# A decoder layer on one core: in every attention step VectorE takes the row maximum ahead of the projections' banks

## The chip, the cores and the metric

The kernel runs on one core of a Trainium2 chip. The metric is the time of one execution on the device in microseconds (us). Inputs and outputs are fp32; matmuls take fp32r operands that are split into a high and a low part.

## The reference, cut to what matters

A decoder layer with pre-norm on x of 8 x 256 x 512: a retention block, then a cross-attention with 32 heads of 16, then a feed-forward with 8 experts and a shared part. The change lies in the cross-attention:

```
q = (x @ Wq).reshape(b, n, N_HEADS, HEAD_DIM)
k, v = jnp.split(ctx @ Wkv, 2, axis=-1)
...
q = apply_axial_rope(q, pos_map)
k = apply_axial_rope(k, ctx_pos_map)
scale = 1.0 / np.sqrt(HEAD_DIM).astype(np.float32)
logits = jnp.einsum('bqhd,bkhd->bhqk', q, k) * scale
w = jax.nn.softmax(logits, axis=-1)
attn = jnp.einsum('bhqk,bkhd->bqhd', w, v)
...
return attn @ Wout + bout
...
x = x + _L0_xattn_ref(_layernorm(x, axis=-1), ctx_1024, fside_BxSx2_0, ...)
```

## The kernel before, in words

The three blocks run one behind the other: retention to about 350 us, cross-attention from 354 to 731 us, feed-forward to the end. The cross-attention walks over the 8 sequences of the batch (g). Each is a pipeline that is spread over several turns: the loop `bodies` runs a body b for b = -1 to 9, and in a body the 16 steps i (T = 16) each do one piece for every sequence b + d with d in -2, -1, 0, 1 that is alive. Every engine has this same loop in its own instruction stream, in its own written order; nothing is planned at run time, and semaphores tie the engines together.

What a step holds on TensorE, in order (line 1290 on): `rows` of head pair p = i of the current sequence (L1185: four matmuls that give the logits with the queries in the partitions, into banks 0 and 1 of `b_rt`; it waits for the maximum of the step before), `logits` of the pair 8 steps back (L1197, transposed logits into banks 2 and 3 for ScalarE's exponential, L1526), the turning of finished values (even steps, L1218), the turning of negated maxima (steps 0, 4, 8, 12, L1224), `values` (odd steps, L1210), and then the projection parts that `PLAN` puts into this step (`use`, L1227).

The projections share two PSUM banks, `b_gm` 0 and 1. In the middle bodies 2 to 6 the order by step, bank in brackets, is: w1 (0) steps 0 to 2, k0 (1) steps 2 and 3, x0 (0) and x1 (1) step 4, k1 (0) step 5, q0 (1) steps 6 to 8, q1 (0) steps 8 to 10, o0 (1) and o1 (0) step 11, v0 (1) step 12, v1 (0) steps 13 and 14, w0 (1) steps 14 and 15. k, q and v are projections of the next sequence, x the transposes of its normalised input, o and w the transposes and the output projection of the sequence before. The first writer of a bank waits on TensorE (L1234) for the semaphore `gm_read` of what was in it before. Body 0 has no o and w, body 1 no w, body 7 no k, x, q and v, and bodies 8 and 9 have no `rows` and no maxima.

A bank is emptied in the step behind its last part: k and q by two VectorE multiplications with the rotation tables (`take`, L1356; `b_ac`, `b_bs`), w by a VectorE addition (L1362), v by ScalarE, and x and o by a ScalarE copy (high part) and then a VectorE subtraction (L1348, low part, `b_xl`), which frees the bank. k0 is so taken in step 4, x0 and x1 in step 5, k1 in 6, q0 in 9, q1 in 11, o0 and o1 in 12, w0 in 0, w1 in 3. Behind the takes of k and q, GpSimd (POOL) sums the products (L1598, L1599), ScalarE makes the high part (L1509), POOL the low part (L1604), and SyncE (SP) sends both to DRAM and loads them again as chunks of rows for the next body.

VectorE's other work in a step stands behind takes and maximum: the negated maxima (steps 3, 7, 11, 15, L1377), the group that scales finished values (even steps, L1386, L1388), statistics (steps 0, 1) and normalisation (steps 2, 3) of the next sequence, and the statistics for the last norm (steps 4, 5, L1396, L1399). In body 0, step 10, a split of weights (`low_weights`, L1469) stands ahead of everything.

Of the kernel before, what the change touches and what calls it, by code (L numbers as in the profile page):

```python
# [32 lines left out]
def as_f32(ap):  # L33

    return ap.bitcast(FP32)
# [929 lines left out]
def cross_attention(nc, X, Wa, Wb, first, csT, wb_dram, ctx_dram, bout_dram, pack_dram, ident, held, final, lead, ws_dram, gate_dram, const_dram, tri_dram):  # L965
# [6 lines left out]
    with ExitStack() as mem:  # L972
# [96 lines left out]
        def due(i, live, step):  # L1069

            return [d for d in live if i - d * T == step]

        def pairs(i, live, lag):
            return [(d, i - d * T - lag) for d in live if 0 <= i - d * T - lag < HP]

        def quads(i, live, lag):
            return [(d, (i - d * T - lag) // 2) for d in live if 0 <= i - d * T - lag < HP and (i - d * T - lag) % 2 == 0]
# [17 lines left out]
        def fresh(g):  # L1095
            return isinstance(g, int) and g <= 0
# [223 lines left out]
        def _(dve):  # L1320

            def bn_first(g):
                nc.vector.bn_stats(out=st[:, 0, :], in_=X[:, g * TB, :])
# [9 lines left out]
            def normalize(g, t):  # L1333
                if t == 0:
                    dve.wait_ge(rstd_done, g)
                last = nc.vector.tensor_scalar(xn[:, t, :], X[:, g * TB + t, :], mv[:, t, 0:1], rstd[:, t:t + 1], ALU.subtract, ALU.mult)
                if t == TB - 1:
                    last.then_inc(xn_done, 1)

            def take(g, what, n):  # L1340

                bank = BANK[what, n]
                src = gm[:, bank, :]
                a = slice(n % 2 * P, (n % 2 + 1) * P)
                if what in ("x", "o"):
                    high, low, done, ahead = (xh, xl, xh_done, 1) if what == "x" else (ah, al, ah_done, 0)
                    dve.wait_ge(done, g * 2 + (n + 1 - 2 * ahead))
                    nc.vector.tensor_tensor(low[:, :, a], src.rearrange("p (m s) -> p m s", s=P), as_f32(high[:, :, a]), ALU.subtract)\  # L1348
                        .then_inc(gm_read[bank], 1)
                elif what in ("k", "q"):  # L1350
                    dve.wait_ge(gm_mm[bank], uses(g, what, n))
                    if not (second(g) and what == "k"):
                        dve.wait_ge(lo_out[n], g * 32 + (-32 if what == "k" else -16))
                    for k, dst in enumerate((ac, bs)):
                        angle = csT[:, k, bass.ts(g, S)].rearrange("p (o s) -> p o s", o=1).to_broadcast([P, 2, S])
                        last = nc.vector.tensor_tensor(dst[:, :, n, :], src.rearrange("p (r s) -> p r s", s=S), angle, ALU.mult)  # L1356
                    last.then_inc(gm_read[bank], 1)
                elif what == "w":
                    dve.wait_ge(gm_mm[bank], uses(g, what, n))
                    dve.wait_ge(bias_added, g + 1)  # L1360
                    tile = X[:, g * TB + n, :]
                    nc.vector.tensor_tensor(tile, src, tile, ALU.add).then_inc(gm_read[bank], 1)  # L1362

            def maximum(g, p):
                dve.wait_ge(row_mm, g * HP + (p + 1))
                nc.vector.tensor_reduce(out=mx[:, :, 2 * p:2 * p + 2].rearrange("p t e -> p e t"),  # L1366
                                        in_=rt[:, 0:2, :].rearrange("p e (t s) -> p e t s", s=S), op=ALU.max, axis=AX.X).then_inc(mx_done, 1)

            def negate(g, k, own):

                dve.wait_ge(mx_done, g * HP + (4 * k + 5))
                part = mx[:, :, 8 * k:8 * k + 8]
                if fresh(g) and k == 0:
                    dve.wait_ge(presets, 3)
                else:
                    dve.wait_ge(mt_mm, g * 4 + k)
                own.step(nc.vector.tensor_scalar(nm[:, :, 0:8].bitcast(FP32R), part, -1.0, None, ALU.mult))  # L1377
                nc.vector.scalar_tensor_tensor(out=nm[:, :, 8:16], in0=part, scalar=-1.0, in1=nm[:, :, 0:8],
                                               op0=ALU.mult, op1=ALU.subtract).then_inc(nm_done, 1)

            def group(g, q, own):

                dve.wait_ge(attn_done, g * 8 + (q + 1))
                dve.wait_ge(nat_done, g * 8 + (q + 1))
                src = nat[:, 0:S].rearrange("p (q d) -> p q d", d=VW)
                own.step(nc.vector.reciprocal(rs[:, :], src[:, :, XD]))  # L1386
                dst = attn[:, :, 64 * q:64 * q + 64].rearrange("p t (h d) -> p t h d", h=4)
                nc.vector.tensor_tensor(dst, src[:, :, 0:XD].rearrange("p (t h) d -> p t h d", t=TB),  # L1388
                                        rs[:, :].rearrange("p (t h o) -> p t h o", t=TB, o=1).to_broadcast([P, TB, 4, XD]),
                                        ALU.mult).then_inc(attn_done, 1)  # L1390
# [19 lines left out]
            def body(b, live):  # L1410
                if isinstance(b, int):
                    own = Chain(dve, dve_own, base=counted["n"])
                else:
                    own = Chain(dve, dve_own, PER, b, counted["n"] - 2 * PER)
                for i in range(T):
                    if isinstance(b, int) and b == 0 and i == 10:
                        low_weights()
                    if isinstance(b, int) and b == B:
                        if i == 0:
                            lead_shift()  # L1420
                        if 6 <= i < 10:
                            lead_low(i - 6)
                    for step, what, n in ENDS:
                        for d in due(i, live, step + 1):
                            if not (fresh(b + d) and step < 0):
                                take(b + d, what, n)
                    for d, p in pairs(i, live, 0):
                        maximum(b + d, p)
                    for k in range(4):
                        for d in due(i, live, 4 * k + 3):  # L1430
                            negate(b + d, k, own)
                    for d, q in quads(i, live, LAGV + 1):
                        group(b + d, q, own)
                    for d in due(i, live, -16):
                        if not fresh(b + d):
                            bn_first(b + d)
                    for d in due(i, live, -15):
                        if not fresh(b + d):
                            statistics(b + d, own)
                    for t in range(TB):  # L1440
                        for d in due(i, live, -14 + t):
                            if not fresh(b + d):
                                normalize(b + d, t)
                    if not (isinstance(b, int) and b > B):
                        for d in due(i, live, 36):
                            final_first(b + d, own)
                        for d in due(i, live, 37):
                            final_statistics(b + d, own)
                if isinstance(b, int):
                    counted["n"] += own.n  # L1450
                else:
                    assert own.n == PER, own.n
                    counted["n"] += (B - 3) * PER

            def lead_shift():
                over(dve)
                dve.wait_ge(frstd_done, 2)
                nc.vector.scalar_tensor_tensor(out=lead.shift_by[:, 0:4], in0=fmean[:, 0:4], scalar=-1.0, in1=frstd[:, 0:4],
                                               op0=ALU.mult, op1=ALU.mult).then_inc(lead.shift_done, 1)

            def lead_low(t):
                dve.wait_ge(lead.xh_done, t + 1)
                at = slice(t * P, (t + 1) * P)
                nc.vector.tensor_tensor(lead.xl[0][:, :, at], gm[:, t % 2, :].rearrange("p (m s) -> p m s", s=P),
                                        as_f32(lead.xh[0][:, :, at]), ALU.subtract).then_inc(lead.xl_done, 1)

            def low_weights():
                dve.wait_ge(wh_done, 1)
                nc.vector.tensor_tensor(wl[:, 2, :], raw[:, :], as_f32(wh[:, 2, :]), ALU.subtract).then_inc(wl_done, 1)  # L1469
# [1097 lines left out]
```

## Time and profile before

| | |
|---|---|
| three runs | 1412.5, 3906.36, 1416.9 us; median 1416.9 |
| the profiled execution | 1415.07 us, its span 1413.3 us |
| mean granted TensorE clock | 0.98 |
| busy in the span | PE 94%, DVE 60%, POOL 36%, ACT 34% |
| from the first `rows` to the end of the cross-attention | 354.27 to 731 us |

Times in the profile are microseconds from the start of the span. PE is TensorE's matmuls, PEld its weight loads, DVE VectorE, ACT ScalarE, POOL GpSimd. In a timeline each line gives the start, the duration from the first start to the last end of the instructions that were merged into it, the engine, the source line, the operation, the output and the inputs. Matmul ends are modelled, so neighbouring matmuls overlap a little in it. A bracket gives the idle time of the engine ahead of the instruction and what ended it.

### The profile page before, as it was taken

How to read it: one execution, taken by the hardware profiler on the slowest of the kernel's cores; microseconds unless marked ns; L12 is line 12 of the kernel's file. 1: busy time of each engine (PE TensorE's matmuls, PEld its weight loads, DVE VectorE, ACT ScalarE, POOL GpSimd, SP SyncE). 2: the span in 40 equal slices, each digit the busy share in tenths (PEclk: the TensorE clock that was granted, in tenths of full speed). 3: DMA queues.
4: the chain of work that ended last, by engine and by line, in shares of the span. 5: the costliest groups of instructions: out<-in, count | busy, mean ns of one | idle time of the engine just before them, and what ended most of it. 6: DMA issues, size and time to landing. Idle time of an engine off the chain costs nothing. (4 is left out here: it accounts for less than half of the span.)

```text
span 1413.3 us, 24145 instructions
## 1 busy us (share of the span) xinstructions
PE 1330.8 (94%) x8442; PEld 1071.2 (76%) x8442; DVE 848.3 (60%) x1519; ACT 486.5 (34%) x764; POOL 508.7 (36%) x359
## 2 busy tenths in 40 slices
PE   7999999998899999999889999999999899999983
PEld 5777777776666766666557888888878899999972
DVE  6766666687888778887744666555561332222255
ACT  4222223243365665565655111111111233332220
POOL 1122222234543344333140028411160775554054
PEclk9999999999799999999999999999999999999997
DMA  7992000003654554456200014220000434452257
GB/s 263 319 323 86 0 0 0 0 16 121 181 165 147 157 165 134 144 148 186 75 24 0 23 41 152 106 94 23 23 23 30 187 138 141 152 201 75 71 154 237
DMA packets 85035, 159.83 MB, mean 113 GB/s; under 512 B 8576, under 2 KB 61952, under 8 KB 81536
## 3 DMA queue, kind: packets, MB, share of 16 engines
q1 hardware_dynamic: 78688, 124.19, 28.0%
q0 software_dynamic: 6272, 34.61, 6.9%
q8 instruction: 51, 0.84, 0.2%
q14 instruction: 24, 0.20, 0.0%
HBM read 109.22 MB, written 69.47 MB: 126 GB/s over the span
## 5 line engine op out<-in xcount | busy, mean ns | idle before, releaser
L1526 ACT ACTIVATE b_pf<-b_rt,b_zero 128x1024 f32<-128x1024 f32 x128 | 142.9, 1116 | 127.3 <-PE b_rt L1197 127.0
L1366 DVE TENSOR_REDUCE b_mx<-b_rt 128x4 f32<-128x1024 f32 x128 | 156.3, 1221 | 47.3 <-PE b_rt L1185 47.2
L2058 DVE SCALAR_TENSOR_TENSOR residual<-c_yp,c_shared,residual 128x512 f32<-128x512 f32 x144 | 103.8, 744 | 114.4 <-PE c_yp L43 108.6
L41 PE MATMUL c_fc<-c_xh,c_w 128*128 128x512 f32 x352 | 137.7, 391 | 0.0
L43 PE MATMUL c_fc<-c_xh,c_w 128*128 128x512 f32 x352 | 137.1, 389 | 0.0
L42 PE MATMUL c_fc<-c_xl,c_w 128*128 128x512 f32 x352 | 137.0, 389 | 0.0
L2196 ACT ACTIVATE c_s<-c_fc 128x512 f32<-128x512 f32 x44 | 26.3, 598 | 231.9 <-PE c_fc L43 220.9
L41 PE MATMUL c_fc<-c_ring,c_xTl 128*128 x312 | 105.3, 338 | 0.0
L43 PE MATMUL c_fc<-c_ring,c_xTh 128*128 x312 | 100.6, 322 | 0.0
L42 PE MATMUL c_fc<-c_ring,c_xTh 128*128 x312 | 100.5, 322 | 0.0
L1878 POOL TENSOR_TENSOR c_w<-c_wraw,c_zero 128x1536 fp32r<-128x1536 f32 x9 | 24.8, 2750 | 202.5 <-DMA c_wraw<-in_c_ws 108.5
L2072 DVE TENSOR_TENSOR c_hTl<-c_eh,c_hTh 128x384 fp32r<-128x384 f32 x39 | 21.7, 557 | 124.2 <-ACT c_hTh L2220 113.1
L1185 PE MATMUL b_rt<-weights_b 50*128 50x256 f32 x512 | 66.8, 340 | 20.4 <-DVE b_mx L1366 19.3
L1898 POOL TENSOR_TENSOR c_ring<-c_eraw,c_zero 128x2816 fp32r<-128x2816 f32 (+1 forms) x16 | 62.9, 3932 | 52.9 <-DMA c_eraw<-in_c_we 52.9
L1185 PEld LDWEIGHTS b_rt<-weights_b 50*128 50x128 f32 x512 | 39.9, 192 | 54.0 <-DVE b_mx L1366 31.4
L1900 POOL TENSOR_TENSOR c_ring<-c_eraw,c_ring 128x2816 fp32r<-128x2816 f32 (+1 forms) x16 | 79.0, 4935 | 1.3
L43 PEld LDWEIGHTS c_fc<-c_xh,c_w 128*128 128x128 f32 x352 | 66.1, 188 | 13.8
L42 PEld LDWEIGHTS c_fc<-c_xl,c_w 128*128 128x128 f32 x352 | 66.1, 188 | 13.5
L41 PEld LDWEIGHTS c_fc<-c_xh,c_w 128*128 128x128 f32 x352 | 66.1, 188 | 13.4
L1210 PE MATMUL b_av<-b_pf,b_vp 128*32 128x256 f32 x1024 | 69.4, 389 | 0.0
L41 PEld LDWEIGHTS c_fc<-c_ring,c_xTl 128*128 128x128 f32 x312 | 58.8, 188 | 6.9 <-issue 5.5
L41 PE MATMUL a_gemm<-weights_a,a_xl 128*128 128x512 f32 x128 | 56.2, 439 | 4.5 <-DVE weights_a L723 2.4
(402 smaller groups left out, 3494.5 us busy)
## 6 DMA issues: line engine op xcount, KB each, us to landing
weights_b<-b_pack SPq DMA_DIRECT2D x128, 200.0 KB
c_eraw<-in_c_we POOLq DMA_DIRECT2D x8, 2176.0 KB, 9.5
b_pack<-b_hi SPq DMA_DIRECT2D x56, 256.0 KB, 2.5
c_rows_in<-in_b_ctx SPq DMA_DIRECT2D x39, 256.0 KB, 9.9
c_rows_out<-in_b_ctx SPq DMA_DIRECT2D x39, 256.0 KB, 10.2
c_xe<-c_rows_in SPq DMA_DIRECT2D x39, 256.0 KB, 3.1
c_rows_out<-c_ye SPq DMA_DIRECT2D x39, 256.0 KB
c_wraw<-in_c_ws SPq DMA_DIRECT2D x11, 768.0 KB, 4.3
```

The source lines that it names most:

```text
L41: nc.tensor.matmul(out, ll, rh, start=start, stop=False)
L42: nc.tensor.matmul(out, lh, rl, start=False, stop=False)
L43: return nc.tensor.matmul(out, lh, rh, start=False, stop=stop)
L1185: last = nc.tensor.matmul(rt[:, e, t * S:(t + 1) * S], qT[r, p, t * P:(t + 1) * P], kT[r, p, :], start=True, stop=True)
L1210: last = nc.tensor.matmul(av[r:r + VW, 0:S], vp[:, j * XH + h, :], pf[:, h % 8, j * S:(j + 1) * S], start=j == 0, stop=j == TB - 1)
L1366: nc.vector.tensor_reduce(out=mx[:, :, 2 * p:2 * p + 2].rearrange("p t e -> p e t"), in_=rt[:, 0:2, :].rearrange("p e (t s) -> p e t s", s ...
L1526: nc.scalar.activation(pf[:, s:s + 2, :], rt[:, 2:4, :], ACT.Exp, scale=XD ** -0.5, bias=zero[:, :]).then_inc(e_done, 1)
L1878: nc.gpsimd.tensor_tensor(w[k][:, 0, :], wraw[k][:, 1, :], zero[:, :].to_broadcast([P, PW]), ALU.add).then_inc(high_done, 1)
L1898: nc.gpsimd.tensor_tensor(high, raw, zero[:, :].to_broadcast([P, hi - lo]), ALU.add).then_inc(high_done, 1)
L1900: nc.gpsimd.tensor_tensor(low, raw, as_f32(high), ALU.subtract).then_inc(ew_done, 1)
L2058: nc.vector.scalar_tensor_tensor(out=X[:, t, :], in0=yp[:, (n * 4 + k) % 3, :], scalar=shared[:, t:t + 1], in1=X[:, t, :], op0=ALU.mult, o ...
L2196: nc.scalar.activation(s[:, n % 2, :], fc[:, n % 2, 0, :], ACT.Silu).then_inc(s_done, 1)
```

## The change

In `body` of VectorE's stream the two loops change places: in each of the 16 steps the maximum of the current head pair is issued first, and the takes that are due in the step are issued behind it. The other engines' streams are as they were.

```
--- before.py
+++ after.py
@@ -1420,12 +1420,12 @@
                             lead_shift()
                         if 6 <= i < 10:
                             lead_low(i - 6)
+                    for d, p in pairs(i, live, 0):
+                        maximum(b + d, p)
                     for step, what, n in ENDS:
                         for d in due(i, live, step + 1):
                             if not (fresh(b + d) and step < 0):
                                 take(b + d, what, n)
-                    for d, p in pairs(i, live, 0):
-                        maximum(b + d, p)
                     for k in range(4):
                         for d in due(i, live, 4 * k + 3):
                             negate(b + d, k, own)
```

## Rows read from the trace of the kernel before

**Rows 1.** Windows: body 3; busy us (instructions) of each engine, granted clock, DMA share, GB/s.

```profile
482.98:528.24 45.26, 43.23 (x405) 31.23 (x404) 36.96 (x70) 26.75 (x39) 18.07 (x19) 1.00 0.51 149
```

**Rows 2.** Waits, cross-attention: who waited for whom, us in total, times, longest.

```profile
DVE b_mx L1366 <- PE b_rt L1185: 47.2, 60, 4.2
...
PE b_rt L1185 <- DVE b_mx L1366: 19.3, 26, 1.4
```

**Rows 3.** Timeline of PE, body 3, steps 4 to 7.

```profile
493.19 0.51 PE L1185 MATMUL b_rt<-weights_b 50*128 50x256 f32 x4
...
494.35 1.17 PE L1239 MATMUL b_gm<-identity,b_xn 128*128 128x128 f32 x8
495.99 0.50 PE L1185 MATMUL b_rt<-weights_b 50*128 50x256 f32 x4 [0.47 <-DVE b_mx L1366]
...
497.90 0.38 PE L41 MATMUL b_gm<-b_ch,weights_a 128*128 128x256 f32 x1 [0.17 <-DVE b_xl L1348]
...
499.63 0.51 PE L1185 MATMUL b_rt<-weights_b 50*128 50x256 f32 x4
...
503.43 0.50 PE L1185 MATMUL b_rt<-weights_b 50*128 50x256 f32 x4 [1.26 <-DVE b_mx L1366]
```

**Rows 4.** Timeline of DVE, body 3, steps 4 to 7.

```profile
493.52 0.69 DVE L1356 TENSOR_TENSOR b_ac<-b_gm,table 128x512 f32<-128x512 f32 x1
494.13 0.68 DVE L1356 TENSOR_TENSOR b_bs<-b_gm,table 128x512 f32<-128x512 f32 x1
494.72 1.22 DVE L1366 TENSOR_REDUCE b_mx<-b_rt 128x4 f32<-128x1024 f32 x1
...
497.16 1.29 DVE L1348 TENSOR_TENSOR b_xl<-b_gm,b_xh 128x512 fp32r<-128x512 f32 x2
498.36 1.22 DVE L1366 TENSOR_REDUCE b_mx<-b_rt 128x4 f32<-128x1024 f32 x1
499.49 0.68 DVE L1399 BATCH_NORM_STATS2 b_fst<-residual 128x6 f32 x1
...
500.95 0.69 DVE L1356 TENSOR_TENSOR b_ac<-b_gm,table 128x512 f32<-128x512 f32 x1
...
503.97 1.23 DVE L1366 TENSOR_REDUCE b_mx<-b_rt 128x4 f32<-128x1024 f32 x1 [0.16 <-PE b_rt L1185]
```

**Rows 5.** Timeline of PE, body 3, steps 11 to 13.

```profile
513.71 0.50 PE L1185 MATMUL b_rt<-weights_b 50*128 50x256 f32 x4
...
514.38 1.07 PE L1210 MATMUL b_av<-b_pf,b_vp 128*32 128x256 f32 x16
515.38 1.09 PE L1268 MATMUL b_gm<-identity,b_attn 128*128 128x128 f32 x8
516.40 0.50 PE L1185 MATMUL b_rt<-weights_b 50*128 50x256 f32 x4
...
517.57 0.50 PE L41 MATMUL b_gm<-weights_a,b_cl 128*128 128x512 f32 x1
...
519.30 0.50 PE L1185 MATMUL b_rt<-weights_b 50*128 50x256 f32 x4
```

**Rows 6.** Timeline of POOL, body 3, step 9: the copy of the values.

```profile
510.92 1.89 POOL L1611 TENSOR_TENSOR b_vp<-b_vn,b_zero 128x1024 f32<-128x1024 f32 x1
```

**Rows 7.** Timeline of PE, body 1, step 5.

```profile
407.06 0.50 PE L1185 MATMUL b_rt<-weights_b 50*128 50x256 f32 x4 [0.48 <-DVE b_mx L1366]
```

**Rows 8.** Timeline of PE, body 0, steps 10 to 13.

```profile
378.73 0.50 PE L1185 MATMUL b_rt<-weights_b 50*128 50x256 f32 x4 [0.23 <-DVE b_mx L1366]
...
382.38 0.50 PE L1185 MATMUL b_rt<-weights_b 50*128 50x256 f32 x4 [0.89 <-DVE b_mx L1366]
...
384.80 0.80 PE L1185 MATMUL b_rt<-weights_b 50*128 50x256 f32 x4 [0.68 <-DVE b_mx L1366]
...
388.96 0.50 PE L1185 MATMUL b_rt<-weights_b 50*128 50x256 f32 x4
```

**Rows 9.** Windows: the 3.2 us from the start of body 0's step 12.

```profile
384.80:388.00 3.20, 3.20 (x15) 2.78 (x16) 2.38 (x5) 1.88 (x3) 0.98 (x3) 0.50 0.33 108
```

More of the change, by code:

```diff
@@ L1422, in body @@
                             lead_low(i - 6)
+                    for d, p in pairs(i, live, 0):
+                        maximum(b + d, p)
                     for step, what, n in ENDS:
@@ L1426, in body @@
                                 take(b + d, what, n)
-                    for d, p in pairs(i, live, 0):
-                        maximum(b + d, p)
                     for k in range(4):
```

## The prediction

> **What bounds the kernel now.** Step n below is turn n of the loop over i. I read the windows of whole bodies first, because the moved lines run only in steps that hold a maximum. Each of the five middle bodies (2 to 6) takes 45.26 us, within 0.02, with TensorE busy 43.2 of them at the full granted clock, VectorE 37.0 and ScalarE 26.8 [rows 1]. So TensorE is the bound, and a moved VectorE instruction counts only where TensorE waits. The list of waits names one pair: over all 128 steps TensorE's row matmuls waited 19.3 us for the maximum of the step before, and the maximum waited 47.2 us for row matmuls [rows 2]. VectorE therefore mostly has time, except in a few steps. The timeline of one middle body shows which: TensorE waits 0.47 us ahead of step 5's row matmuls, 0.17 us ahead of k1 in step 5 and 1.26 us ahead of step 7's [rows 3]. On VectorE these are the steps where a take of two instructions (pitch 1.2 us) or a pair of lows stands ahead of the maximum [rows 4]. Everything else in the body starts back to back.
>
> **What the change does.** No instruction is added or removed, and no duration changes: a maximum stays 1.22 us (the next instruction follows after 1.13), two takes 1.2 us. Where a step holds both, the maximum now starts when its row matmuls are done, 0.54 us after their start (503.43 [rows 3] to 503.97 [rows 4]), and the takes start behind it. Two things follow. The next row matmuls are released earlier. The bank of the take is free later, and a bank's next writer may be a matmul of the same step. By the plan and the order of the banks that is so at four places: x1's transposes in step 4 wait for k0's take, k1 in step 5 waits for x0's low, o1's transposes in step 11 wait for q1's take, and v0 in step 12 waits for o0's low. TensorE issues in order, so all that is behind such a writer waits too, the next row matmuls first.
>
> **A middle body, step by step**, on the clock of the body shown.
> Step 4: row matmuls at 493.19 [rows 3]; VectorE is free at 493.7 (w1's take now stands behind the maximum of step 3, which gives normalisation 0.2 us later), so the maximum runs 493.75 to 494.98 and k0's take 494.88 to 496.17, where it ended at 494.81 [rows 4]. x0's transposes start at 494.35 and take half of the 1.02 us that eight take (515.38 to 516.40) [rows 5]; x1's start at 496.22 and end TensorE's step at 496.8. Step 5's row matmuls come at 496.8 against 495.99: +0.8. The wait of 0.47 is gone and one of 1.35 has come.
> Step 5: group and first statistics of the final norm take VectorE to 497.4; maximum 497.4 to 498.6; x0's low ends at 499.2. k1 could start 1.67 us behind the row matmuls, at 498.5 (as the o transposes do in step 11, 513.71 to 515.38 [rows 5]), and starts at 499.25. From its start to the next row matmuls it is 1.73 us, 0.11 of them a wait for the maximum [rows 3], so 1.62: step 6 at 500.87 against 499.63, +1.24.
> Step 6: x1's low ends at 499.8 and the final statistics, 1.46 us (499.49 to 500.95) [rows 4], at 501.2, before the row matmuls are done at 501.4. The maximum runs 501.4 to 502.64, k1's take behind it. TensorE's own step is 3.80 less 1.26, near 2.5 us: step 7 at 503.35 against 503.43, −0.1. This is the whole win of the change, 1.26 of waiting, and it pays the loss of steps 4 and 5.
> Steps 7 to 10: k1's take ends at 503.8, 1.6 us later; the maximum of step 7 ends at 505.5, step 8 comes at 505.9. q0's take in step 9 has no writer waiting in its step. POOL's sum of q0 comes 2.1 us later, and POOL's copy of the values, 1.89 us from 510.92 [rows 6], ends near 514.9. The value matmuls of step 11, 0.67 behind the row matmuls [rows 5], want it at 514.3: 0.6 us of waiting, which the next place hides.
> Step 11: row matmuls at 513.61; maximum 514.15 to 515.38, q1's take to 516.57. o0's transposes are done at 516.46 (515.79 without POOL's wait); o1's start at 516.62, half a microsecond long: step 12 at 517.15 against 516.40 [rows 5], +0.75.
> Step 12: maximum 517.7 to 518.9; o0's low to 519.5. v0, 1.17 us behind its row matmuls in the trace, could start at 518.3 and starts at 519.55; to the next row matmuls it takes 1.59 us (1.73 less the 0.14 that step 13 waited for its maximum): step 13 at 521.14 against 519.30 [rows 5], **+1.84**.
> Steps 13 to 3: the take of w0 (0) has no waiting writer, the maximum of step 1 moves 0.2 us and step 1 has room. So a middle body costs 1.84, five of them 9.2 us.
>
> **The other bodies.** Body 1 has the same four places, but no final statistics, so there is nothing to win at step 7: its step 5 waited 0.48 us [rows 7]. +1.4 at step 7, and +1.95 for steps 11 and 12: +3.4. Body 0 has the places of steps 4 and 5, at half clock, and none in 11 and 12 (no o). It waited 0.23, 0.89 and 0.68 us for maxima in steps 10 to 12 [rows 8]; the 0.68 is won, the 0.89 is low_weights, which stands ahead of both and now begins behind q0's take. I take +3.0 between the 0.8 of step 4 alone and 5 if the low clock at its start lasts one stretch longer. Body 7 has no k, q or x. Its o lows hold step 13 back, but VectorE's own work of steps 12 and 13 is the same in either order, and step 14 comes at the same time; what is won in step 4 is taken by the DMA of the maxima, which `logits` waits for there. 0. Bodies 8 and 9 have no maxima.
> The projection's chain behind the takes (POOL sum, ScalarE high, POOL low, SP's DMA, chunk load) is 1.2 to 2.1 us later. SP is moved past nothing, and the first chunk of the next head is issued near 519 instead of 517.9, wanted at 530: covered. If that cover is gone, row matmuls wait for a chunk, at most by those 2 us a body.
> **Sum:** 9.2 + 3.4 + 3.0 + 0 = 15.6. The profiled execution took 1415.07 us, so 1430.7; the median of the runs is 1.8 above it, 1416.9, so I forecast **1432** for a median. The feed-forward part behind follows its start one for one, as TensorE is its chain.
>
> **Rivals.**
> A, not slower: the banks are freed in time anyway, and only the release of the row matmuls counts. For it: the waits list names the maximum as what ends TensorE's waits [rows 2], and the takes' transposes waited nowhere in the trace. It gives −(0.47 + 0.17 + 1.26) x 5 and about 1.2 in bodies 0 and 1: −10.7, 1406. Against it: k0's take and the maximum must both fit ahead of x1's transposes, and 1.2 + 1.2 us do not fit into the 1.2 from row matmuls to them. The Trainium skill says in Perfetto Trace Analysis, Optimization Strategies, that when the matmul engine idles one should "optimize those engines that are blocking the critical path"; by it the maximum would go first and the time would be this rival's. The rows speak against it, for the take blocks as well. Chance 0.10.
> B, part of it: one pair of places (steps 4 and 5, or 11 and 12) costs little, because ScalarE's copy or VectorE's start differs from mine by half a microsecond. The win of 1.26 and a loss of 1.2, or 1.24 + 0 at 11 and 12, leave +2 to +9: 1418 to 1425. 0.12.
> C, slower by more: TensorE's new idle time lets its clock fall. In body 0 the engine waited 0.89 and 0.68 us in steps 11 and 12 [rows 8], and then the granted clock is 0.50 for 3.2 us, 1.2 GHz of 2.4 [rows 9]; step 12 took 4.16 us where a middle body takes 2.90 [rows 5, 8]: 1.3 us a fall. A single wait of 1.26 let nothing fall [rows 3]. The new waits are 1.35 and 0.77 in steps 4 and 5, and 0.6, 0.16 and 1.3 in steps 11 and 12, near the case that fell. From one fall in each of six bodies the time is 1440, with two 1448; from here it decides. The Trainium skill, same page, Matmul Optimizations, wants matmuls "back-to-back in batches" since power follows use; the row at 0.50 agrees. 0.13.
> The forecast itself: 1426 to 1438, chance 0.60; 0.05 for what I do not see.
>
> **Numbers.** The range 1420 to 1445 holds the forecast, C with up to one and a half falls, and B's upper part: about 0.8. A measurement of this kernel can tell about 2% from no change, which is 28 us, 1389 or 1445. Faster by over 2% 0.01, slower 0.06 (C with two falls), within 0.93.
>
> **What would show it.** In a middle body of the changed kernel: period 47.1 us; ahead of x1's transposes a wait for b_bs of 1.3 us, ahead of k1 one for b_xl of 0.8, ahead of o1 and v0 two more; no wait of 1.26 ahead of step 7; POOL's sums later. Were the waits for b_mx gone and no waits for b_bs and b_xl there, A is right; slices at 0.50 in the middle bodies show C; a wait of row matmuls for a DMA shows that the chunk's cover is gone.

## The result, and the profile after

The changed kernel takes 1433.28 us (median of four runs, 1430.80 to 1436.90) against 1419.74 us for four runs of the kernel before. One of these four took 3906.36 us; the ratio leaves it out (the median of the other three is 1416.9 us). The ratio is 1.0119, 95% interval [1.0083, 1.0156]: slower, by less than 2%. The profiled execution took 1431.72 us with a span of 1429.9; before it was 1415.07 and 1413.3. The difference of the spans, 16.6 us, can be laid out by the first row matmuls (L1185) of each body:

| stretch | before | after | difference | forecast |
|---|---|---|---|---|
| start of the span to body 0 | 354.27 | 352.41 | -1.9 | 0 |
| body 0 | 41.00 | 45.39 | +4.4 | +3.0 |
| body 1 | 42.43 | 45.79 | +3.4 | +3.4 |
| bodies 2 to 6 | 226.35 | 236.18 | +9.8 | +9.2 |
| body 7, to its last row matmuls | 35.78 | 36.90 | +1.1 | 0 |
| from there to the end | 713.47 | 713.23 | -0.2 | 0 |

The first line holds nothing that the change touches: the same stretch ends between 352.3 and 354.1 in the kernels below, whatever their order.

The window of body 3, with the columns of [rows 1]:

```profile
490.81:538.05 47.24, 43.37 (x406) 31.34 (x406) 37.38 (x70) 27.18 (x39) 18.03 (x19) 1.00 0.48 143
```

TensorE is as busy as before (43.4 against 43.2 us) and its clock is full; the body is 1.98 us longer, so the difference is waiting. The list of waits over the cross-attention (here to 748 us, where it ends in this trace) tells who is waited for, and answers to [rows 2]:

```profile
DVE b_mx L1366 <- PE b_rt L1185: 77.8, 88, 4.5
POOL b_ac L1598 <- DVE b_bs L1356: 76.8, 28, 4.4
...
PE b_gm L41 <- DVE b_xl L1348: 11.9, 13, 1.1
...
PE b_gm L1239 <- DVE b_bs L1356: 8.7, 7, 1.3
...
PE b_rt L1185 <- DVE b_mx L1366: 7.4, 12, 1.3
...
PE b_av L1210 <- POOL b_vp L1611: 4.8, 7, 0.8
```

The row matmuls wait 7.4 us for the maximum where it was 19.3: the change does what it says. In its place TensorE waits 11.9 us for the lows of x and o (1.9 before), 8.7 for k0's take and 4.8 for POOL's copy of the values (neither before). Within bodies 2 to 6 alone TensorE's listed waits add up to 19.4 us against 9.6, and the difference of 9.8 is the whole loss of these bodies. VectorE itself waits more than before (77.8 against 47.2): it now stands idle for the row matmuls while takes lie behind it in its queue.

The timeline of TensorE in body 3, steps 4 to 7, answers to [rows 3]:

```profile
501.02 0.51 PE L1185 MATMUL b_rt<-weights_b 50*128 50x256 f32 x4
...
502.19 0.60 PE L1239 MATMUL b_gm<-identity,b_xn 128*128 128x128 f32 x4
504.05 0.66 PE L1239 MATMUL b_gm<-identity,b_xn 128*128 128x128 f32 x4 [1.26 <-DVE b_bs L1356]
504.63 0.51 PE L1185 MATMUL b_rt<-weights_b 50*128 50x256 f32 x4
...
507.09 0.39 PE L41 MATMUL b_gm<-b_ch,weights_a 128*128 128x256 f32 x1 [0.72 <-DVE b_xl L1348]
508.72 0.50 PE L1185 MATMUL b_rt<-weights_b 50*128 50x256 f32 x4
...
511.19 0.50 PE L1185 MATMUL b_rt<-weights_b 50*128 50x256 f32 x4
```

The eight transposes of x, one line of before, are two groups of four with 1.26 us between them; k1 waits 0.72; the 1.26 ahead of step 7 is gone. Steps 4, 5 and 6 take 3.61, 4.09 and 2.47 us, where they took 2.80, 3.64 and 3.80.

VectorE in the same steps, for [rows 4]:

```profile
501.57 1.23 DVE L1366 TENSOR_REDUCE b_mx<-b_rt 128x4 f32<-128x1024 f32 x1
502.71 0.68 DVE L1356 TENSOR_TENSOR b_ac<-b_gm,table 128x512 f32<-128x512 f32 x1
503.31 0.68 DVE L1356 TENSOR_TENSOR b_bs<-b_gm,table 128x512 f32<-128x512 f32 x1
...
505.21 1.23 DVE L1366 TENSOR_REDUCE b_mx<-b_rt 128x4 f32<-128x1024 f32 x1
506.35 1.28 DVE L1348 TENSOR_TENSOR b_xl<-b_gm,b_xh 128x512 fp32r<-128x512 f32 x2
```

The take of k0 ends at 503.99 and x1's transposes start at 504.05. And TensorE in steps 11 to 13, for [rows 5]:

```profile
521.48 0.50 PE L1185 MATMUL b_rt<-weights_b 50*128 50x256 f32 x4
...
523.01 1.07 PE L1210 MATMUL b_av<-b_pf,b_vp 128*32 128x256 f32 x16 [0.80 <-POOL b_vp L1611]
524.02 1.14 PE L1268 MATMUL b_gm<-identity,b_attn 128*128 128x128 f32 x8
525.09 0.50 PE L1185 MATMUL b_rt<-weights_b 50*128 50x256 f32 x4
...
527.51 0.50 PE L41 MATMUL b_gm<-weights_a,b_cl 128*128 128x512 f32 x1 [1.10 <-DVE b_xl L1348]
529.11 0.51 PE L1185 MATMUL b_rt<-weights_b 50*128 50x256 f32 x4
```

Step 11 takes 3.61 us (2.69 before), step 12 takes 4.02 (2.90). In step 11 the wait stands ahead of the values, for POOL's copy. It makes the o transposes so late that q1's take is nearly done by then: o1's follow o0's almost at once, in one line of 1.14 us. The copy of [rows 6] ends 1.29 us behind the row matmuls of step 11, where it ended 0.9 us ahead of them:

```profile
520.87 1.90 POOL L1611 TENSOR_TENSOR b_vp<-b_vn,b_zero 128x1024 f32<-128x1024 f32 x1
```

### The profile page after: what moved, and what is told of

Same layout as the page of the kernel before. It is cut to its first block and busy times, and to the rows that moved or that the text cites. A ratio compares the mean times of both kernels' runs of the same rounds, so it can differ in the third digit from the quotient of the medians.

```text
span 1429.9 us, 24145 instructions
## 1 busy us (share of the span) xinstructions
PE 1332.7 (93%) x8442; PEld 1072.0 (75%) x8442; DVE 855.0 (60%) x1519; ACT 489.3 (34%) x764; POOL 509.2 (36%) x359
## 5 line engine op out<-in xcount | busy, mean ns | idle before, releaser
L1366 DVE TENSOR_REDUCE b_mx<-b_rt 128x4 f32<-128x1024 f32 x128 | 156.7, 1224 | 78.9 <-PE b_rt L1185 77.8
L1185 PE MATMUL b_rt<-weights_b 50*128 50x256 f32 x512 | 67.0, 341 | 7.5 <-DVE b_mx L1366 7.4
L1185 PEld LDWEIGHTS b_rt<-weights_b 50*128 50x128 f32 x512 | 39.9, 193 | 39.6 <-issue 20.6
```

The source lines that it names most:

```text
L1185: last = nc.tensor.matmul(rt[:, e, t * S:(t + 1) * S], qT[r, p, t * P:(t + 1) * P], kT[r, p, :], start=True, stop=True)
```

## The experiments

The theory: a take that stands behind the maximum frees its bank later, and four writers of the same step (x1, k1, o1, v0) pay for it. Counted from the row matmuls of the step, k0's take ends 1.35 us later than before (2.97 against 1.62), and k1 and v0, which wait for a low, start 0.55 and 1.25 us later. The rivals: only the release of the row matmuls counts; POOL's late copy, not the bank, holds step 11; the loss comes from VectorE being full. Since whole executions differ by some us, the main measure is the period of a middle body and its steps, from one row matmul to the next; in bodies 2 to 6 of one trace they agree within 0.1 us unless told. Steps 4, 5, 6, 11 and 12 of body 3:

| kernel | 4 | 5 | 6 | 11 | 12 | body 3 |
|---|---|---|---|---|---|---|
| before | 2.80 | 3.64 | 3.80 | 2.69 | 2.90 | 45.26 |
| changed | 3.61 | 4.09 | 2.47 | 3.61 | 4.02 | 47.24 |
| e1 | 3.61 | 4.07 | 2.77 | 2.69 | 2.90 | 45.48 |
| e2 | 2.80 | 3.65 | 3.79 | 3.60 | 3.99 | 47.32 |
| e3 | 2.94 | 3.64 | 2.52 | 3.55 | 2.90 | 45.41 |
| e4 | 3.60 | 4.09 | 2.47 | 3.61 | 4.01 | 47.25 |
| e7 | 2.81 | 3.29 | 2.59 | 2.69 | 2.90 | 43.70 |
| e9 | 3.60 | 4.06 | 2.47 | 3.60 | 4.03 | 47.20 |
| e10 | 2.93 | 3.65 | 2.52 | 2.69 | 3.30 | 44.89 |

**e1: maximum first in steps 4 and 5 alone.** The same edit serves e2 with (11, 12) and e3 with the other twelve steps.

```
+                    early = i in (4, 5,)
+                    if early:
+                        for d, p in pairs(i, live, 0):
+                            maximum(b + d, p)
                     for step, what, n in ENDS:
...
+                    if not early:
+                        for d, p in pairs(i, live, 0):
+                            maximum(b + d, p)
```

> The kernel before, with the maximum first in steps 4 and 5 alone. Theory (same-step bank writers): a middle body's step 4 takes 3.6 us (2.80 before), step 5 4.1 (3.64), and step 6, where the take is still first, about 2.8 (3.80), since the maximum there then starts behind k1's take; period 45.5 us against 45.27. Body 1 +1.4, body 0 +4. In all +6 to +7 us. Rival (only the release of the row matmuls counts): period 44.6 us, total -4 us.

Measured: step 4 3.61, step 5 4.07, step 6 2.77, period 45.5; ratio 1.0043 [1.0012, 1.0075], near 6 us. Body 1 grew by 1.43 us, as expected, body 0 by 2.7 where I expected 4. TensorE's waits in body 3:

```profile
500.26 0.66 PE L1239 MATMUL b_gm<-identity,b_xn 128*128 128x128 f32 x4 [1.26 <-DVE b_bs L1356]
503.30 0.38 PE L41 MATMUL b_gm<-b_ch,weights_a 128*128 128x256 f32 x1 [0.72 <-DVE b_xl L1348]
507.69 0.50 PE L1185 MATMUL b_rt<-weights_b 50*128 50x256 f32 x4 [0.24 <-DVE b_mx L1366]
```

The two bank waits are those of the changed kernel to the hundredth, with nothing else of the change in place. They also push the next row matmuls back, so that most of the wait ahead of step 7 is gone (0.24 of 1.26) though the take is first there. The cost of steps 4 and 5, 1.24 us, and that gain nearly cancel: +0.2 a body. The rival (44.6) is out.

**e2: maximum first in steps 11 and 12 alone.**

> The kernel before, with the maximum first in steps 11 and 12 alone. Theory: step 11 grows from 2.69 to near 3.4 us, or 2.7 + 0.9 if POOL's copy of the values is no part of it (here q0's take is early, so it is not late), step 12 from 2.90 to 4.0; period 47.2 us, waits ahead of o1's transposes (0.9) and of v0 (1.1). Bodies 1 to 6 +1.9 each, total +11.5 us. Rival (step 11's loss in the changed kernel is POOL's late copy): step 11 stays near 2.7, period 46.4, total +6.5.

Measured: step 11 3.60, step 12 3.99, period 47.3; ratio 1.0113 [1.0059, 1.0166], near 16 us with a wide interval, where 11.5 was expected. In the trace bodies 1 to 6 cost 2.1 us each, but for one. The waits of body 3 in these steps:

```profile
517.49 0.66 PE L1268 MATMUL b_gm<-identity,b_attn 128*128 128x128 f32 x4
518.85 0.66 PE L1268 MATMUL b_gm<-identity,b_attn 128*128 128x128 f32 x4 [0.70 <-DVE b_bs L1356]
521.86 0.51 PE L41 MATMUL b_gm<-weights_a,b_cl 128*128 128x512 f32 x1 [1.09 <-DVE b_xl L1348]
```

Here q0's take is early, POOL's copy is in time, and the wait stands ahead of o1's transposes instead. So the bank alone makes step 11 3.60. This pair of steps is nearly the whole loss of the change in a middle body: nothing behind it gives time back. The one body (5) took 48.71 us, of which more below.

**e3: maximum first in all steps but 4, 5, 11 and 12.**

> The kernel before, with the maximum first in all steps but 4, 5, 11 and 12. Theory: no writer waits for a take in its own step; the wait of 1.26 ahead of step 7's row matmuls goes nearly whole, and w1's take behind the maximum in step 3 costs 0.1 to 0.2 in step 4. Period 44.1 to 44.3 us, total -5 to -6 us. Rival (any take behind a maximum delays TensorE, as the chain POOL, ScalarE, SP behind it gets late): period 45.3 or more, total 0 or above.

Measured: the wait ahead of step 7 is gone (step 6 2.52), but the period is 45.4, not 44.2; ratio 0.9987 [0.9959, 1.0014], no difference. My expectation failed, and the rival (the chain behind the take gets late) came true:

```profile
514.33 1.07 PE L1210 MATMUL b_av<-b_pf,b_vp 128*32 128x256 f32 x16 [0.79 <-POOL b_vp L1616]
```

With q0's take behind the maximum of step 9, POOL's sum and the copy behind it come late, and this alone makes step 11 3.55 (e10 below shows it). Steps 7 and 8 lose 0.2 each, both through k1's take, which stands behind the maximum of step 6. In step 7 the next maximum comes late behind this take: it ends at 504.86, and the row matmuls of step 8 start at 504.91. In step 8 POOL's sum is late, ScalarE waits 0.77 us for it ahead of its high part, and behind this stands the copy of finished values that TensorE wants to turn: it ends at 505.71 and the turning starts at 505.76. So a take has a second customer, the chain of POOL and ScalarE, beside the bank's next writer.

**e4: the changed kernel, POOL's copy ahead of its sum.**

```
+                    for d in due(i, live, 9):
+                        copy_values(b + d)
                     for n, step in enumerate(SUMS):
...
-                    for d in due(i, live, 9):
-                        copy_values(b + d)
```

> The changed kernel, with POOL's copy of the values ahead of its sum of q0 in step 9, so that the copy is done when step 11's value matmuls want it. Theory (both hold step 11, the later one counts): the wait of 0.80 ahead of the values goes, and one of 0.8 to 0.9 for b_bs appears ahead of o1's transposes; step 11 stays at 3.6 us, period 47.2. Rival (POOL's copy alone is step 11's loss): step 11 falls to 2.8, period 46.4.

Measured: step 11 3.61, period 47.25 (one execution, as for e5, e6 and e8 to e10).

```profile
524.16 0.66 PE L1268 MATMUL b_gm<-identity,b_attn 128*128 128x128 f32 x4
525.51 0.66 PE L1268 MATMUL b_gm<-identity,b_attn 128*128 128x128 f32 x4 [0.70 <-DVE b_bs L1356]
```

The wait for POOL goes, the one for q1's take comes, and the step is as long. Both hold it, and the later one is seen in the trace.

**e10: e3 with e4's edit.**

> e3_first_elsewhere with POOL's copy of the values ahead of its sum of q0. Theory (there the late copy alone holds step 11): step 11 2.7 instead of 3.55, period 44.5. Rival (q0's late sum holds ScalarE's high part and with it the values too): step 10 or 11 grows, period 45 or more.

Measured: step 11 2.69, as expected; step 12 grew to 3.30, so the period is 44.9. This closes step 11: with neither cause it is 2.69, with the copy alone 3.55 (e3), with the bank alone 3.60 (e2, e4), with both 3.61. The trace also shows what added 0.4 to step 12:

```profile
515.78 0.74 POOL L1604 TENSOR_TENSOR b_ac<-b_bs,b_ac 128x256 f32<-128x256 f32 x1
515.90 0.66 DVE L1378 SCALAR_TENSOR_TENSOR b_nm<-b_mx,b_nm 128x16 f32<-128x16 f32 x1
...
516.48 1.27 DVE L1348 TENSOR_TENSOR b_xl<-b_gm,b_xh 128x512 fp32r<-128x512 f32 x2
...
517.21 0.50 PE L41 MATMUL b_gm<-weights_a,b_cl 128*128 128x512 f32 x1 [0.16 <-DVE b_xl L1348]
```

The second half of the negation falls beside POOL's second sum of q1 and takes 0.66 us; in the kernel before it starts at 516.67, when that sum is over, and takes 0.18. So the lows of o start 0.84 us behind the row matmuls of step 12 (at 515.64) instead of 0.42, and v0 starts 1.57 us behind them instead of 1.17. This is read from the trace and not tested by a run.

**e5 and e6: q1 finished one step earlier,** on the changed kernel, without and with e4's edit.

```
-                (-8, "q", 1, (0,)), (-7, "q", 1, (1,)), (-6, "q", 1, (2, 3)),
+                (-8, "q", 1, (0,)), (-7, "q", 1, (1, 2, 3)),
```

> The changed kernel, with q1's last matmuls in step 9 instead of 10, so that its take falls into step 10 and bank 0 is free when o1 wants it. Theory (POOL's late copy and the bank each hold step 11 by itself): the wait of 0.80 for POOL stays, step 11 stays near 3.55 us; step 9 grows by 0.7 and step 10 shrinks by as much; period 47.2. Rival (the bank alone): step 11 falls to 2.8, period 46.4.

> Both at once on the changed kernel: q1 finished in step 9 and POOL's copy of the values ahead of its sum of q0. Theory: only now is step 11 free, 2.7 us, period 46.3; no wait for b_vp and none for b_bs ahead of o1. Rival (something third holds step 11): 3.3 us or more.

Both missed what they were for. The edit moves 12 matmuls, 1.43 us, not the 0.7 I wrote. Step 9 became 4.01 and step 10 1.82, at whose end the row matmuls of step 11 waited 0.72 us for the maximum; the copy was then in time in either kernel. Step 11 fell to 2.77 in both, steps 9 to 11 together stayed at 8.6, and step 12 grew to 4.24: period 47.4 and 47.5, but for one body of 48.9 in each. They say only that with o1's bank free step 11 is short, and decide nothing between copy and bank.

**e8: k0 finished one step earlier,** on the changed kernel.

```
-                (-14, "k", 0, (0,)), (-13, "k", 0, (1,)),
+                (-14, "k", 0, (0, 1)),
```

> The changed kernel, with all of k0's matmuls in step 2, so that its take falls into step 3 and bank 1 is free when x1 wants it in step 4. Theory (bank and full VectorE): the wait of 1.26 ahead of x1 goes, step 4 falls from 3.61 to 3.0, but VectorE's queue of steps 3 to 5 is as long as before, so x0's low comes at the same time, k1 waits 1.3 instead of 0.72 and steps 4 and 5 together stay at 7.7. Rival (bank waits alone, each its own price): steps 4 and 5 together 7.1, period 46.6.

Measured: periods 48.9 to 50.0, 1445.65 us. Body 5, whose clock stayed full:

```profile
609.59 0.44 PE L1224 MATMUL b_av<-identity,b_nm 128*128 128x128 f32 x2 [1.52 <-DVE b_nm L1378]
610.62 1.06 PE L1239 MATMUL b_gm<-identity,b_xn 128*128 128x128 f32 x8 [0.59 <-DVE b_xn L1336]
...
614.71 0.39 PE L41 MATMUL b_gm<-b_ch,weights_a 128*128 128x256 f32 x1 [1.30 <-DVE b_xl L1348]
```

The wait ahead of x1 went and k1's grew to 1.30, as I wrote. But steps 4 and 5 of this body together took 9.37 us, not 7.7. I had left out that the negated maxima and the normalisation stand behind the takes in step 3: their turning waits 1.52 and x0's transposes 0.59 us more. The take was not too late at its place, it was in the way at another.

**e7: the kernel before, statistics of the last norm moved** out of VectorE's full steps. The rest is the kernel before.

```
-                        for d in due(i, live, 36):
+                        for d in due(i, live, 45):
                             final_first(b + d, own)
-                        for d in due(i, live, 37):
+                        for d in due(i, live, 46):
                             final_statistics(b + d, own)
...
-                        for d in due(i, live, 38):
+                        for d in due(i, live, 47):
                             final_root(b + d)
```

> The kernel before, takes first as it has them, with the statistics of the last norm moved from steps 4, 5 (and their root from 6) to steps 13, 14 (15). Theory (the 1.26 ahead of step 7 is VectorE being full from step 4 to 6, not its order): step 5 3.3 us instead of 3.64, step 6 2.5 instead of 3.80, period 43.6 instead of 45.27, no wait for b_mx ahead of step 7 and nothing late behind the takes; in all -8 us, ratio 0.994. Rival (POOL's or ScalarE's chain holds step 6 as well): period 44.6 or more.

Measured: period 43.7, steps 5 and 6 3.29 and 2.59; 1402.43 us against 1409.57 for the kernel before on the same chip (the experiments ran on three chips, so times compare only within a pair), ratio 0.9945 [0.9919, 0.9970]. TensorE has one wait left in body 3:

```profile
491.56 0.50 PE L1185 MATMUL b_rt<-weights_b 50*128 50x256 f32 x4 [0.48 <-DVE b_mx L1366]
```

The wait that the change was able to remove, 1.26 us ahead of step 7, needs both causes: the take ahead of the maximum, and 2.3 us of statistics ahead of both. Either alone can be taken away (step 6 is 2.52 in e3, which moves the take, and 2.59 here), but moving the statistics leaves the banks free in time. This version is faster than the kernel before by 0.5%, clear of the noise though under 2%; its middle body is 3.5 us shorter than that of the changed kernel.

**e9: the changed kernel with e7's edit.**

> The changed kernel with the statistics of the last norm moved as in e7_stats_moved. Theory (the bank waits follow from the order alone, not from a full VectorE): step 4 stays 3.6, step 5 4.1, step 6 2.5, step 11 3.6, step 12 4.0; period 47.2 as in the changed kernel, so the order costs 3.5 us a body against the 43.7 of e7. Rival (the change loses because VectorE is full): period 45.5 or less.

Measured: period 47.2, steps 3.60, 4.06, 2.47, 3.60, 4.03. Relieving VectorE wins 1.6 us a body with the takes first and nothing with the maximum first. So the order costs 3.5 us a body once VectorE has room, against 2.0 in the kernels compared: the full VectorE hid a part of the loss, and made none of it.

## Why the prediction was right, point by point

**The total.** 1432 was forecast and 1433.3 measured, inside 1420 to 1445; against 1416.9 the forecast is +1.1%, and the measured ratio is +1.2%. Part of the closeness is luck: bodies 0 and 7 cost 2.5 us more than forecast and bodies 2 to 6 another 0.6, and the stretch before the attention, 1.9 us shorter in this execution, offset most of it.

**The four writers of the same step.** Right, each step with its size: step 4 3.61 against 3.61 in my working, step 5 4.09 against 4.07, step 6 2.47 against 2.5, step 11 3.61 against 3.54, step 12 4.02 against 3.99. e1 and e2 show the two pairs apart. One sign did not come: a wait ahead of o1. My working gave it 0.16 us behind 0.6 for POOL's copy; POOL's wait was 0.80 and took it in, and only with the copy in time (e2, e4) does o1 wait, 0.70. v0's wait was 1.10 where the working has 1.25. That matmuls behind a waiting writer wait too is seen in each. The Trainium skill says the same in PSUM — Partial Sum Buffer, Engine vs sequencer instructions: matmuls start and complete in program order.

**The win at step 7 pays for steps 4 and 5.** Right: steps 4 to 6 take 10.17 us against 10.24. e7 adds what the forecast did not look for: this win was to be had without the loss.

**POOL's copy, "0.6 us of waiting, which the next place hides".** The mechanism was right, the size 0.80, and e4 shows that either wait hides the other. I then did not carry it to e3, where the next place is gone and the copy costs 0.86 us a body by itself.

**Body 1.** It cost 3.36 us where 3.4 was forecast.

**Body 0.** Forecast +3.0 with bounds 0.8 and 5, measured +4.4. The term was mis-sized. Steps 4 and 5 cost 3.4 us (5.17 and 5.60 against 3.75 and 3.59), and steps 8 to 12, from which the forecast took a win of 0.68, cost 0.9. At half clock x1's transposes waited 1.15 us; k1's wait, which ends with x0's low and is filed under "issue", was 2.0:

```profile
PE b_gm L41 <- issue: 2.0, 1, 2.0
PE b_rt L1197 <- ACT b_pf L1526: 1.6, 2, 1.2
PE b_av L1224 <- DVE b_nm L1378: 1.4, 2, 0.8
PE b_gm L1239 <- DVE b_bs L1356: 1.1, 1, 1.1
```

The second and third rows were in no term: ScalarE's exponentials, late in steps 9 and 10, and the negated maxima, 0.55 us late in step 4 and, behind q1's take in step 11, 0.82 in step 12. The largest part behind step 5 is step 10, 5.23 us against 3.65. The wait of 0.89 for the maximum is gone, but `logits` now waits for ScalarE's exponential, which stands behind ScalarE's own copy of weights (1.90 us from 379.39):

```profile
382.35 0.80 PE L1197 MATMUL b_rt<-weights_b 50*128 50x256 f32 x4 [1.21 <-ACT b_pf L1526]
```

Behind this wait TensorE runs at half clock: the matmuls of q1 follow each other at 0.21 us, in the kernel before at 0.12. In e3, e4 and e10, where the maximum stands first in steps 9 and 10 too, step 10 takes 5.1 to 5.3 us, and 3.66 in e1, e2 and e7, where it does not. In e9 the wait was the same (1.22) and the clock stayed full: step 10 took 4.26.

**Body 7.** Forecast 0, measured +1.1. The order itself cost nothing, as forecast: what step 12 won (1.83 us against 2.76) step 13 gave back (2.77 against 1.83). That the DMA of the maxima takes what is won in step 4 held too: the row matmuls waited 0.18 us for the maximum instead of 0.51, and `logits` waited 2.53 us for the DMA instead of 1.99. What had no term is the clock. Before, it fell within this wait (slices of 2 us at 0.50 from 675 to 681); here it was still 1.00 when the wait ended, fell about 1 us later, and the slices at 0.50 reach from 694 to 702. Step 7, at full clock before, ran at half and took 3.01 us instead of 1.92. That it was the longer wait that moved and lengthened the low stretch is argued, not shown; in e5 and e6, with the same order, body 7 took 35.8 us as before, and in the other kernels from 34.65 to 39.49.

**Rival C, the clock.** In the changed kernel no middle body saw a fall (granted clock 1.00 from 440 to 680), so it did not decide. But it is real: in e2 one body of the five took 48.71 us instead of 47.3, in e4 one took 48.55, in e5 and e6 one each took 48.91, and e8 has slices below 1.00 in several. The windows of that body in e4, three stretches of 5 us:

```profile
615.00:620.00 5.00, 4.30 (x49) 3.08 (x45) 4.12 (x7) 3.63 (x5) 3.35 (x4) 1.00 0.58 159
620.00:625.00 5.00, 3.90 (x21) 2.98 (x22) 3.56 (x7) 2.50 (x5) 2.70 (x3) 0.75 0.50 160
625.00:630.00 5.00, 5.00 (x43) 3.00 (x42) 2.24 (x2) 2.76 (x4) 0.00 (x0) 0.91 0.84 251
```

The clock goes to half behind the waits of 0.69 us ahead of o1 and 1.10 ahead of v0, and the body is 1.3 us longer, the price of a fall that the forecast took from body 0 before.

## What to carry to other kernels

Where one engine both feeds a chain and empties banks, ask for every bank who writes it next and in which step, before changing the order: a take that seemed to have a step's time had none, as the bank's next writer stood in the same step. The name of what ends a wait says which instruction came last, not which one is to be moved; here the waits named the maximum, and the remedy was to move 2.3 us of statistics that no matmul of these steps waits for. And a late take has more than one customer: the bank's writer and POOL's chain were each enough to hold step 11.

## What the runs showed of the hardware that was not expected

A VectorE instruction of 0.17 us became one of 0.72 when POOL began beside it. In step 11 of body 3 of the changed kernel the second half of the negation (two inputs in SBUF) starts 0.04 us behind POOL's sum:

```profile
524.36 0.17 DVE L1377 TENSOR_SCALAR b_nm<-b_mx 128x16 fp32r<-128x16 f32 x1
524.52 0.73 POOL L1598 TENSOR_TENSOR b_ac<-b_ac,b_bs 128x256 f32<-128x256 f32 x1 [0.52 <-DVE b_bs L1356]
524.56 0.72 DVE L1378 SCALAR_TENSOR_TENSOR b_nm<-b_mx,b_nm 128x16 f32<-128x16 f32 x1
```

Its median over 32 is 176 ns, so it ends with POOL's instruction rather than by its own work. The Trainium skill says in SBUF — State Buffer, Who interferes with whom, that a VectorE instruction with two SBUF inputs contends with a GpSimd instruction that reads SBUF; this row agrees. The same happens in e8 (0.71 us), where it puts the normalisation back, and in e10 (0.66 us), where it adds 0.4 us to step 12. The first half of the negation, whose one tile input is `b_mx`, was stretched beside POOL too: it took 0.58 us in step 11 of body 3 of e3 and ended at 516.04, with POOL's sum at 516.00. In body 0 of the changed kernel the second half took 1.19 us beside a POOL addition of 2.50, and this is the 0.55 us that the turning waited in step 4. In the changed kernel the order brings the two together: the take that releases POOL's sum now stands right ahead of the negation.

The clock fell behind two waits of 0.70 and 1.10 us, 2.6 us from start to start, in one body of five, and behind the same two waits in the other four it did not (e2, e4 alike). In e5 and e6 it fell behind waits of 0.72 and 1.29 us, again in one body of five. Behind the waits of the changed kernel and of e9 (near 1.26, 0.7, 0.80 and 1.10 us in a middle body) it fell in none of ten bodies.
